# A packed word for the tile numbers of sixteen items, loaded by TensorE for two groups at a time, in a three-layer graph attention kernel

## What is computed

```python
def gatv2(x, src, dst, n, Wl, Wr, att, b):          # layers 0 and 1, H=4, C=64
    xl = (x @ Wl).reshape(n, H, C)
    xr = (x @ Wr).reshape(n, H, C)
    e = leaky_relu(xl[src] + xr[dst], 0.2)
    logits = einsum('ehc,hc->eh', e, att)
    m = segment_max(logits, dst, n)
    ex = exp(logits - m[dst])
    denom = segment_sum(ex, dst, n)
    alpha = ex / (denom[dst] + 1e-16)
    return segment_sum(xl[src] * alpha[:, :, None], dst, n).reshape(n, H * C) + b
```

## Time and profile before

| | us |
|---|---|
| runs before: median (lowest to highest) | 3970.88 (3966.65 to 3974.2) |
| the profiled execution: own time | 3967.72 |
| its span, first to last instruction | 3965.9 |
| TensorE matmul, weight load | 3516.9, 2584.0 busy |
| VectorE, GpSimd, ScalarE | 3298.3, 2743.8, 1273.7 busy |
| mean granted TensorE clock | 0.957 of full speed |

### The profile page before, as it was taken

One profiled execution on the slowest core, in us unless ns is written; L12 is line 12 of the kernel. 1 busy time (PEld: TensorE's weight loads), 2 busy tenths in 40 slices (PEclk: granted clock), 3 DMA queues, 4 the chain that ended last, 5 costly groups with the idle time before them and its releaser, 6 DMA issues. The chain is left out here.

```text
span 3965.9 us, 115129 instructions
## 1 busy us (share of the span) xinstructions
PE 3516.9 (89%) x30761; PEld 2584.0 (65%) x30762; DVE 3298.3 (83%) x9999; ACT 1273.7 (32%) x4356; POOL 2743.8 (69%) x3039
## 2 busy tenths in 40 slices
PE   7799999999999669999999999977678877878776
PEld 5577777777776446777777777745455555555544
DVE  7788888888888885888888888875688888888887
ACT  4433333333333553333333333324111111111113
POOL 5777777777775557777777777723777777777760
PEclk9999999999999899999999999989789999999899
DMA  4444444444443225444444444435445555555544
GB/s 116 133 131 137 135 131 137 135 135 131 137 134 87 68 72 146 130 137 135 133 134 136 135 131 138 130 97 183 134 137 145 144 142 144 140 144 145 142 123 130
DMA packets 279448, 520.88 MB, mean 131 GB/s; under 512 B 98430, under 2 KB 165160, under 8 KB 279352
## 3 DMA queue, kind: packets, MB, share of 16 engines
q0 software_dynamic: 120320, 338.39, 31.5%
q1 hardware_dynamic: 148096, 177.74, 14.6%
q10 hardware_dynamic: 10936, 3.62, 0.5%
HBM read 484.05 MB, written 35.46 MB: 131 GB/s over the span
## 5 line engine op out<-in xcount | busy, mean ns | idle before, releaser
L706 POOL DMA_INDIRECT gathered<-table,idx x2496 | 2480.5, 994 | 809.1 <-issue 550.6
L1143 PE MATMUL pS<-gathered,Dm 128*128 128x264 f32 x4992 | 1692.1, 423 | 106.4 <-DVE Dm L1557 57.8
L1544 DVE TENSOR_TENSOR acc_mem<-acc_mem,pS 128x264 f32 x2496 | 1045.5, 419 | 144.8 <-PE pS L1143 109.6
L1082 PE MATMUL pZ<-DT,x 128*128 128x128 bf16 x9984 | 1092.4, 221 | 15.2 <-DVE DT L1504 11.3
L1082 PEld LDWEIGHTS pZ<-DT,x 128*128 x9984 | 874.8, 99 | 326.2 <-issue 53.5
L891 ACT ACTIVATE reluT<-pZ 128x256 f32<-128x256 f32 x1664 | 636.7, 383 | 1128.5 <-PE pZ L1088 1114.7
L1143 PEld LDWEIGHTS pS<-gathered,Dm 128*128 128x128 f32 x4992 | 799.7, 201 | 236.6 <-DVE gathered L1575 104.5
L1088 PE MATMUL pZ<-ident,gathered 128*128 128x128 f32 x3328 | 936.4, 281 | 12.4 <-DMA gathered<-table,idx 12.2
L1575 DVE TENSOR_TENSOR gathered<-gathered 128x256 f32<-128x256 f32 x2496 | 942.9, 418 | 2.3 <-ACT gathered L881 1.1
L1557 DVE TENSOR_TENSOR Dm<-pS,rel_items 128x256 f32<-128x256 f32 x1239 | 514.8, 415 | 0.0
L1088 PEld LDWEIGHTS pZ<-ident,gathered 128*128 128x128 f32 x3328 | 471.2, 142 | 16.2 <-DMA gathered<-table,idx 14.9
(11 more groups left out here) (242 smaller groups left out, 3214.1 us busy)
## 6 DMA issues: line engine op xcount, KB each, us to landing
DT<-rel_dram SPq DMA_DIRECT2D x156, 512.0 KB
gathered<-table,idx POOLq DMA_INDIRECT x2496
table<-xls SPq DMA_DIRECT2D x147, 132.0 KB, 1.8
flags<-flag_dram SPq DMA_DIRECT2D x416, 32.0 KB
flags<-flag_dram SPq DMA_DIRECT2D x52, 256.0 KB
gathered<-table SPq DMA_DIRECT2D x98, 132.0 KB, 2.1
gathered<-in_x SPq DMA_DIRECT2D x98, 128.0 KB, 2.2
hx_dram<-gathered SPq DMA_DIRECT2D x49, 128.0 KB, 1.8
```

Source lines behind the costliest of these rows:

```text
L706: nc.gpsimd.indirect_dma_start(out=G[:, b, i, :], out_offset=None, in_=tab[l], in_offset=bass.IndirectOffsetOnAxis(ap=idx[:, b, i:i + 1], ...
L1082: mm = nc.tensor.matmul(z_slot(i)[:, half], x3[:, bass.ds(tk[i], 1), s, half].rearrange("p o c -> p (o c)"), moving, start=(s == 0), stop= ...
L1143: nc.tensor.matmul(pS[:, i % 4, 0:ROW], Dm[:, i % 8, :], G[:, at[0], at[1], :], start=True, stop=True).then_inc(seg_done, 1)
L1544: link(v.tensor_tensor(acc_at(n), acc_at(n), pS[:, n % 4, 0:ROW], ALU.add))
```

## The change

The tile numbers of a group's 16 items go into one word: the tile of its first item, shifted left by 16 bits, and 15 bits (of 16) of which bit i - 1 says whether item i is in the next tile. VectorE builds the words in the preamble and in seven steps at tiles 16 to 22 of node stage 0, by doubling the distance in four passes of multiply and add. They lie in `t_words` in pairs: the b = 1 word of a group pair and the b = 0 word of the next. TensorE loads a pair by one register load at each b = 1 group, and works out the tiles from it: item 0 by a shift, folded into the first address as a divide, item i as the tile before plus one bit. The loads on TensorE go from 624 to 81 (3 layers x 27). 29 register operations a group are added: one for item 1, two for each of items 2 to 15.

```diff
@@ -91,6 +91,8 @@
         rel_items = sb("rel_items", [P, ITEMS])
         last_items = sb("last_items", [P, ITEMS], BF16)
         t_row = sb("t_row", [1, ITEMS], I32)
+        CELLS = NG // 2 + 1
+        t_words = sb("t_words", [1, CELLS, 2], I32)
         ident = sb("ident", [P, P])
         iota_row = sb("iota_row", [P, P])
         iota_part = sb("iota_part", [P, 1])
@@ -164,6 +166,9 @@
         zsum = small[:, 0:2, :]
         small = small.rearrange("p (s b) k -> p s b k", s=4)
         assert g_at[0] <= 2 * GI * ROW
+        WORDS = ITEMS + GI
+        assert WORDS <= 4 * D and TILES << 16 < 1 << 24
+        t_of, step_a, step_b = (a.rearrange("p a c -> p (a c)")[0:1, 0:WORDS] for a in (own, res, nd))
         xls = sb("xls", [P, 2, ROW])
         pool_pad = sb("pool_pad", [P, 8])
 
@@ -218,6 +223,7 @@
         pre_flag = sem("pre_flag")
         pre_idx = sem("pre_idx")
         pre_acc = sem("pre_acc")
+        words_step = sem("words_step")
 
         w_in = sem("w_in")
         att_in = sem("att_in")
@@ -404,6 +410,19 @@
         def static(v):
             return isinstance(v, int)
 
+        def load_words(engine, cell, col, n):
+
+            return list(nc.values_load_multi_w_load_instructions(
+                t_words[0:1, bass.ds(cell, 1), col:col + n].rearrange("p o c -> p (o c)"), engines=(engine,), min_val=0, max_val=(TILES << GI) - 1,
+                skip_runtime_bounds_check_because="a word holds a tile number and 16 bits by construction")[1])
+
+        def first_tile(eng, word):
+            return eng.snap((word >> GI).with_bounds(min_val=0, max_val=TILES - 1))
+
+        def next_tile(eng, word, tile, n):
+
+            return eng.snap((tile + ((word >> n) & 1)).with_bounds(min_val=0, max_val=TILES - 1))
+
         def per_h(ap, H):
 
             return ap[:, 0:GI * H].rearrange("p (h i) -> p i h", h=H)
@@ -720,8 +739,10 @@
         def _(act):
 
             act.wait_ge(pre_pe, 2)
+            act.wait_ge(pre_v, PV_COL)
             for b in range(NB):
-                ins = nc.scalar.activation(t_row[0:1, b * BS:(b + 1) * BS], pX[0:1, b // FB, (b % FB) * BS:(b % FB + 1) * BS], ACT.Copy)
+                nc.scalar.activation(t_row[0:1, b * BS:(b + 1) * BS], pX[0:1, b // FB, (b % FB) * BS:(b % FB + 1) * BS], ACT.Copy)
+                ins = nc.scalar.activation(t_of[0:1, b * BS:(b + 1) * BS], pX[0:1, b // FB, (b % FB) * BS:(b % FB + 1) * BS], ACT.Copy)
             ins.then_inc(pre_act, 1)
             def indices(t, b, h):
 
@@ -1046,24 +1067,22 @@
                 up, settle, state = tally()
                 settled = {3: wg_done, 4: added, 5: relu_done, 7: scan_done, 9: carry_ready, 10: dif_ready, 11: dt_ready, 12: fx_ready, 13: lin_ready,
                            14: logits_copied}
+                words = [None, None]
 
                 def body(gh, b, first, second, late):
-                    k0 = (gh * 2 + b) * GI
                     c = 1 - b
                     here = pe.snap(landed_need(l, gh)) if first and l < 2 else None
                     tk = []
 
-                    def load_tiles():
-
-                        tk.extend(nc.values_load_multi_w_load_instructions(
-                            t_row[0:1, bass.ds(k0 + len(tk), 4)], engines=(PE,), min_val=0, max_val=TILES - 1,
-                            skip_runtime_bounds_check_because="t_k is a tile number by construction")[1])
-
-                    if first:
-                        load_tiles()
+                    if first and b == 1:
+                        words[:] = load_words(PE, gh + 1, 0, 2)
+                    elif first and not second:
+                        words[:] = load_words(PE, 0, 0, 2)
+                    word = words[1 - b]
 
                     def expand(i, freed):
 
+                        tk.append(next_tile(pe, word, tk[-1], i - 1) if i else first_tile(pe, word))
                         if i == 0:
                             pe.wait_ge(dt_ready, up(dt_ready))
                         if l < 2 and i % Q != 1 and (second or i >= 2):
@@ -1141,8 +1160,6 @@
                             if i % 2 and not closing:
                                 pe.wait_ge(wg_done, up(wg_done))
                             nc.tensor.matmul(pS[:, i % 4, 0:ROW], Dm[:, i % 8, :], G[:, at[0], at[1], :], start=True, stop=True).then_inc(seg_done, 1)
-                        if first and i % 4 == 3 and i + 1 < GI:
-                            load_tiles()
                         if b == 0 and i in settled:
                             settle(pe, settled[i])
                     if not second and b == 1:
@@ -1185,6 +1202,10 @@
             v.tensor_copy(ones_row[:], ident[:, 0:1].to_broadcast([P, P]))
             dve.wait_ge(pre_pe, 1)
             pre(v.tensor_copy(ki[0:BS, 0, 0:NB], pM[0:BS, 0:NB]))
+            v.memset(t_of, 0.0)
+            v.memset(step_a, 0.0)
+            v.memset(step_b, 0.0)
+            v.memset(t_words[:], 0)
             pre(v.tensor_copy(kf[0:BS, 0:NB], ki[0:BS, 2, 0:NB]))
             pre(v.tensor_tensor(kf[0:BS, 0:NB], kf[0:BS, 0:NB], pM[0:BS, 0:NB], ALU.subtract), PV_COL)
             tcol = cols[0:BS, 0:NB]
@@ -1195,10 +1216,38 @@
             v.memset(spans[:], -BIG)
             v.memset(end_row[:], -BIG)
 
+            n_words = [0]
+
+            def words_link(ins):
+                n_words[0] += 1
+                ins.then_inc(words_step, 1)
+                dve.wait_ge(words_step, n_words[0])
+
+            def tile_words(step):
+
+                last = ITEMS - 1
+                if step == 0:
+                    dve.wait_ge(pre_act, 1)
+                    words_link(v.tensor_tensor(step_a[:, 0:last], t_of[:, 1:last + 1], t_of[:, 0:last], ALU.subtract))
+                elif step <= 4:
+                    far, span = 1 << (step - 1), WORDS - (1 << step) + 1
+                    frm, to = (step_a, step_b) if step % 2 else (step_b, step_a)
+                    words_link(v.scalar_tensor_tensor(to[:, 0:span], frm[:, far:far + span], float(1 << far), frm[:, 0:span], ALU.mult, ALU.add))
+                elif step == 5:
+                    words_link(v.scalar_tensor_tensor(step_b[:, 0:WORDS - GI], t_of[:, 0:WORDS - GI], float(1 << GI), step_a[:, 0:WORDS - GI],
+                                                      ALU.mult, ALU.add))
+                else:
+                    pairs = NG // 2
+                    for col, cell, at_k, n in ((0, 1, GI, pairs), (1, 0, 0, pairs)):
+                        ins = v.tensor_copy(t_words[0:1, cell:cell + n, col], step_b[:, at_k:at_k + 2 * GI * (n - 1) + 1:2 * GI])
+                    words_link(ins)
+
             def indices(t, b, h):
 
                 if not static(t):
                     return
+                if OWN + 10 <= t < OWN + 17:
+                    tile_words(t - OWN - 10)
                 if t == OWN:
                     dve.wait_ge(pre_gather, 32 * NB)
                     pre(v.tensor_copy(dstf, g_dst))
```

## The result

The change made the kernel slower: 4012.28 us median (4011.16 to 4015.51) against 3972.23, a ratio of 1.0102 with a 95% interval of 1.0087 to 1.0117. The forecast was 3977 and its range ended at 3992, so the time lies outside it. The profiled execution took 4011.16, its span is 4009.3 against 3965.9.

The account below looks back on a forecast made before the run. TensorE with its sequencer was taken to bound layers 0 and 1, gathers layer 2. On 3967.72, +1.0 (layers 0 and 1), +2.3 (preamble) and +2.7 (node stage 0) gave 3973.7; on the median of runs before, 3977; range 3954 to 3992.

Parts of the forecast that it names:

- The bound: TensorE with its sequencer sets the pace in layers 0 and 1, GpSimd close behind; gathers set it in layer 2.
- Item 8: Removing the load after item 7, ahead of item 8, saves 0.22 us a group, -0.44 a pair of groups.
- Item 6: Its two register operations come after the wait for `dif`, 2 x 0.09: +0.18 us a group, +0.36 a pair.
- first rival: Item 6's operations run while `dif` is waited for, so 0.36 us a pair goes: 3958; chance 0.15.
- third rival: VectorE's `dif` comes sooner, so the load after item 3 counts, up to 0.2 us a group, -21: 3956; chance 0.10.
- the start of the b = 1 group: Behind the loop's branch, item 15's two operations add 0.18 us a pair; the load of two words gains 0.08.
- second rival: Sequencer doesn't get ahead within item 6; item 7's two operations cost +0.18 us a group, +19: 3996; chance 0.15.
- Each operation: A register operation on TensorE's sequencer costs between 0.032 and 0.12 us, taken as 0.09.
- The preamble: Three memsets of 848 elements ahead of VectorE's index work delay TensorE's first node tile: +2.3 us, bounds 1.5 and 2.9.
- Node stage 0: Seven VectorE steps at tiles 16 to 22, partly covered by idle gaps: +2.7 us, bounds 0 and 6.3.

Follow-up runs that it names:

- the kernel with the words alone: Words built as in the changed kernel, TensorE's whole program that of the kernel before with its 624 loads; 3975.61 us against 3970.11, ratio 1.0016.

## Why the prediction was wrong

**The bound** was read rightly: TensorE with its sequencer in layers 0 and 1, gathers in layer 2, which took 2.8 us more of 1082; that isn't more than layer 2 varies between the runs (1079 to 1085).

**Item 8**: forecast -0.44 a pair. Items 7 and 8 gave back 0.315 in both groups, net of the 0.03 to 0.05 by which their own operations now show. Right in kind, a little large.

**Item 6**: forecast +0.36 a pair. Behind `dif` 0.133 and 0.140 were added before item 6's first load, and 0.068 and 0.094 inside it: 0.43. Right. The operations did not run ahead while `dif` was waited for, so the first rival falls: in all 40 groups of the 20 pairs the first of them starts within 0.001 us of L1122's weight load, and `relu_done`, the only thing that item 6 itself waits for, had come 2 us earlier. By the Trainium skill's rule ("Advanced Engine Details and Errata", Sequencer Loop) they could have; these runs don't agree with it at this place. The third rival falls nearly whole: `dif` came earlier by 0.10 a pair, where that rival had up to 0.2 a group, which is why items 3 to 6 together show +0.335 and not +0.43.

**The step that failed is the start of the b = 1 group**, "+0.18 for item 15's two operations, -0.08 for the shorter load", +0.10 forecast and +0.572 measured. It was two errors.
- The load. I let the duration go with the number of words, from half of 0.33 to all of it. It rose to 0.54: +0.205 by experiment, outside my bounds, since I had taken it that fewer words cannot cost more.
- The lead. I counted item 15's operations alone and put those of items 9 to 14 at 0, as they "have the same cover, TensorE's own 1.01 us an item". But the sequencer takes 1.12 us for an item of b = 0 with two operations, TensorE 1.01, so each such item eats 0.1 of the lead and the branch finds what is left of it: 0.30 us at item 15, where it was 0.62. Without the operations of items 12 to 15 0.349 came back, twice my 0.18. The second rival named the condition (the sequencer's own time for an item with two operations "passes 1.01 us") and put its price at item 7, where it is small; I gave it 0.15 and looked at one item where the debt runs over several.

**Each operation** was taken at 0.09 and is 0.097, with 0.013 more in the next address.

**The preamble**: forecast 2.3, measured 2.7 at TensorE's first node tile, and 2.6 by experiment. Right at that place.

**Node stage 0**: forecast 2.7, measured 4.55 (3.0 in the kernel with the words alone). VectorE's groups there, 70 to 95 us, in the changed kernel:

```profile
L1485 DVE TENSOR_TENSOR gathered<-xls,gathered 128x256 f32<-128x256 f32 x7 | 4.9, 701 | 2.8 <-ACT x L834 2.7
L1235 DVE SCALAR_TENSOR_TENSOR gathered<-gathered 1x847 f32<-1x847 f32 (+3 forms) x4 | 4.1, 1017 | 0.0
```

The passes took 1.02 each, close to the forecast 1.0, and all that was added is 6.4. The idle time before the first step of a tile fell from 6.4 to 2.8, which is 3.6 of cover, about as much as I had taken. But the first steps themselves (L1485, L1436 before) are shown as 4.9 long in all where they were 3.5, and that 1.4 I hadn't counted: 6.4 - 3.6 + 1.4 = 4.2. Why they take longer when they follow at once isn't shown. The size is within the bounds.

In sum: 50 steady pairs at +0.58 give 29, against my +1; what was forecast as 5 for the preamble and node stage 0 came as 7; layer 2 and the later node stages are 3 longer, and some 4 are left in layers 0 and 1. These last stand in the second pair of groups of layer 1, which took 49.9 us where it was 44.4. They aren't chance of one execution: that pair takes 48.2 to 49.9 in all six kernels that have two operations ahead of each of the items 2 to 15, and 42.9 to 46.0 in the other eight. Most of it is at item 15 ahead of the first round of the loop, 3.6 us over its steady value against 1.0 before. Why it comes there isn't shown.

## What to carry to other kernels

Price a sequencer by its balance over a stretch, not by the instruction: add up its time for each item, compare it with the engine's, and follow the lead up to the next load, branch or unsatisfied wait, where whatever was used up is paid at once. Before trading register loads for arithmetic, look at where the loads stand; here moving two in every four was worth 14 us, while replacing 543 of the 624 by arithmetic cost 40. And when a chain has several engines within a few per cent of each other, expect what you free to be taken by the next one.

## What was not expected of the hardware

A register load of two int32 by TensorE takes 0.53 to 0.56 us and one of four 0.33 to 0.35 us, in both buffers, behind a branch or not (312 and 468 loads in one kernel, 81 and 81 in two others, the first load of each program apart). I can't say why; one and three were not tried. The first load of a program takes 0.19 more (0.514 to 0.516 of four, 0.722 of two). A register operation that follows another on TensorE's sequencer starts 0.097 us after it in most cases, though it is shown as 0.036 long, and a semaphore count given back costs some 0.14 us of the sequencer's time (1.12 against 0.99 us an item).
